# Attention phase: the last context row as a per-channel constant on x, its double stored once, and the weight fold ahead of the sums with x

## The reference, cut to what matters

```python
qf = jnp.fft.fft(q, axis=2); kf = jnp.fft.fft(k, axis=2)        # q = layernorm(x), k = v = ctx
corr = jnp.fft.ifft(qf * jnp.conj(kf), axis=2).real
w, idx = jax.lax.top_k(corr.transpose(0, 1, 3, 2), topk)        # topk = 11 delays per channel
w = jax.nn.softmax(w, axis=-1)
for i in range(topk):
    g = jnp.minimum(idx[:, :, None, :, i] + pos, L - 1)          # past the end: the last row again
    out = out + w[:, :, None, :, i] * jnp.take_along_axis(v, g, axis=2)
x = x + out
```

## Time and profile before

| | before |
|---|---|
| time, median of 3 runs | 3191.58 us (3190.05 to 3197.46) |
| the profiled execution | 3189.48 us, its span 3187.7 us |
| attention phase | the first 1220 us or so of the span |
| PE, DVE, ACT, POOL busy, whole span | 91%, 86%, 71%, 50% |
| granted clock of TensorE, whole span | 0.972 |

### The profile page before, as it was taken

One profiled execution on the slowest core, in us unless ns is written; L12 is line 12 of the kernel. 1 busy time (PEld: TensorE's weight loads), 2 busy tenths in 40 slices (PEclk: granted clock), 3 DMA queues, 4 the chain that ended last, 5 costly groups with the idle time before them and its releaser, 6 DMA issues. The chain is left out here.

```text
span 3187.7 us, 47981 instructions
## 1 busy us (share of the span) xinstructions
PE 2911.0 (91%) x13554; PEld 1586.1 (50%) x13554; DVE 2737.9 (86%) x7168; ACT 2252.5 (71%) x5963; POOL 1581.7 (50%) x1161
## 2 busy tenths in 40 slices
PE   5999999999999996899999999999999999738886
PEld 3666666666666663445444454444445444322322
DVE  4999999999999996776878879787887978769996
ACT  6888888888888862765766767667586766468773
POOL 5999999999999992001212121121212212016776
PEclk8999999999999998999999999999999999859998
DMA  5555555555555535354654737465473744553664
GB/s 174 185 188 167 180 174 161 181 173 160 178 178 160 177 117 173 87 163 126 177 169 136 225 110 214 131 178 163 136 225 103 206 148 132 124 194 147 247 250 162
DMA packets 272044, 532.26 MB, mean 167 GB/s; under 512 B 32664, under 2 KB 132760, under 8 KB 248992
## 3 DMA queue, kind: packets, MB, share of 16 engines
q1 hardware_dynamic: 245600, 422.17, 42.4%
q10 hardware_dynamic: 15168, 71.34, 7.9%
q0 software_dynamic: 11008, 35.66, 3.3%
HBM read 401.07 MB, written 128.02 MB: 166 GB/s over the span
## 5 line engine op out<-in xcount | busy, mean ns | idle before, releaser
L1065 PE MATMUL acc<-xh,wq 128*128 128x512 f16 x4096 | 1205.7, 381 | 46.3 <-DVE x_first L1722 17.1
L1065 PE MATMUL acc<-xl,wq 128*128 128x512 f16 x2048 | 758.9, 380 | 0.0
L1284 ACT ACTIVATE unused<-c_first,minus_guess 128x256 bf16<-128x256 f32 x1024 | 505.2, 494 | 268.5 <-DVE minus_guess L1596 224.5
L1065 PEld LDWEIGHTS acc<-xh,wq 128*128 128x128 f16 x4096 | 399.4, 98 | 532.9 <-DVE x_first L1722 23.3
L994 POOL DMA_DIRECT2D c_first<-ctx_pairs x120 | 66.5, 554 | 857.3 <-DVE mk L1647 846.9
L1065 PEld LDWEIGHTS acc<-xl,wq 128*128 128x128 f16 x2048 | 200.8, 98 | 243.3 <-issue 2.7
L444 PEld LDWEIGHTS bu<-m_iz,zf 128*128 128x128 f32 x2048 | 278.9, 191 | 50.3 <-issue 35.6
L444 PE MATMUL bu<-m_iz,zf 128*128 128x128 f32 (+2 forms) x2048 | 293.0, 301 | 5.5 <-DVE zf L648 5.5
L463 PE MATMUL bx<-m_ic,pf 128*128 128x256 f32 x1024 | 236.1, 384 | 8.9 <-POOL pf L345 8.9
L463 PEld LDWEIGHTS bx<-m_ic,pf 128*128 128x128 f32 x1024 | 192.7, 193 | 34.1 <-POOL pf L345 9.7
L1266 ACT ACTIVATE unread<-cf 128x256 bf16<-128x256 f32 x256 | 106.1, 415 | 127.9 <-DVE feat_pair L1695 94.9
(11 more groups left out here) (359 smaller groups left out, 6975.9 us busy)
## 6 DMA issues: line engine op xcount, KB each, us to landing
wq<-w_split SPq DMA_DIRECT2D x512, 256.0 KB, 3.2
c_first<-ctx SPq DMA_DIRECT2D x64, 512.0 KB, 7.4
xt<-xT SPq DMA_DIRECT2D x64, 512.0 KB, 5.9
x_pairs<-xo SPq DMA_DIRECT2D x64, 512.0 KB, 3.3
c_first<-ctx_pairs POOLq DMA_DIRECT2D x128, 256.0 KB, 4.8
x<-xn_pairs SPq DMA_DIRECT2D x32, 1024.0 KB, 5.4
out_pairs<-ost SPq DMA_DIRECT2D x32, 1024.0 KB, 5.1
x_first<-x SPq DMA_DIRECT2D x15, 2048.0 KB, 8.4
```

What stands on the lines that cost most here:

```text
L1065: return pe.matmul(acc[b][:], ws[(WQ * o + k // CK) % WR][:, k % CK, a, :], x[:, k, :], start=start, stop=False)
L1284: act.activation(signs[:, u // 2, t] if n == COUNTS - 1 else unused[u % 2][:], ct[k % CR][:, t], ACT.Sign, bias=guess[q % 2][:, u:u + 1], ...
```

## The change

The constant that the last row adds to the even part is the same at every time and the weights of a channel sum to one, so it comes out as v_last / 2 on every output of the channel. The changed kernel leaves it out of the spectrum and adds it to x: ScalarE adds a column `lc` (128 partitions, one column per group of 128 channels) to the tile `xt` in four instructions per chunk (`add_last`). The doubled last rows are made once at the start from a new input, stored to a scratch array `last` in DRAM and loaded from there per chunk straight into `vl2`. On VectorE the folds of the weights move ahead of the sums with x; on ScalarE the copy `w_back` moves ahead of the row sums of the weights and both correlation copies move ahead of the squares.

```diff
@@ SyncE, at the start @@
+            sp.dma_start(lr[:], last_in_rows).then_inc(last_in, 16)
+            sp.dma_start(lc[:], last_cols).then_inc(cols_in, 16)
...
+            sp.wait_ge(last_ok, 1)
+            sp.dma_start(last.rearrange("b (a n) -> (b a) n", a=P // NB), lr[:]).then_inc(last_out, 16)
@@ SyncE, each chunk @@
-                        sp.wait_ge(vl2_ok, n_scaled)
-                        sp.wait_ge(ce_ok, n_folded)
-                    sp.dma_start(vl[s][:], ctx[bass.ds(b, 1), L // 2, c * CW:(c + 1) * CW].rearrange("a n -> (a n)").partition_broadcast(P)).then_inc(vl_in[s], 16)
+                        sp.wait_ge(eo_ok, h - 1)
+                        sp.wait_ge(ce_ok, 2 * (h - 1))
+                    else:
+                        sp.wait_ge(last_out, 16)
+                    sp.dma_start(vl2[s], last[bass.ds(b, 1), c * CW:(c + 1) * CW].rearrange("a n -> (a n)").partition_broadcast(P)).then_inc(vl_in[s], 16)
@@ GpSimd, the odd fold @@
-                pool.wait_ge(vl2_ok, h + 1)
+                pool.wait_ge(vl_in[s], 16 * (4 * it + kk // 2 + 1))
@@ TensorE, ahead of the transposes @@
-                        pe.wait_ge(dc_ok, f + 1)
+                        pe.wait_ge(k_sb, f + 1)
@@ ScalarE @@
+            act.wait_ge(last_in, 16)
+            act.activation(lr[:], lr[:], ACT.Copy, scale=2.0).then_inc(last_ok, 1)
+            act.wait_ge(cols_in, 16)
+            act.activation(lc[:], lc[:], ACT.Copy, scale=0.5).then_inc(cols_ok, 1)
+            act.wait_ge(cols_ok, 1)
...
-                act.activation(vl2[s][:], vl[s][:], ACT.Copy, scale=2.0).then_inc(vl2_ok, 1)
+                tile = xt[kk % 2]
+                act.wait_ge(xt_in[kk % 2], 16 * (4 * it + kk // 2 + 1))
+                for j in range(CT):
+                    act.activation(tile[:, j, :], tile[:, j, :], ACT.Identity, bias=lc[:, CT * g + j:CT * g + j + 1]).then_inc(xt_ok, 1)
...
+                if k % CH in (1, 2):
+                    add_last(it, k)
...
+                if k % CH not in (1, 2):
+                    add_last(it, k)
@@ VectorE @@
-                    dve.wait_ge(k_part, 3 * f + 2)
-                    dve.scalar_tensor_tensor(kf[s][0:1, 0, :], vl2[s][0:1, :], L / 2.0, by[0:1, 0, :], ALU.mult, ALU.add).then_inc(dc_ok, 1)
...
+                    for j in range(CT):
+                        dve.wait_ge(xt_ok, CT * g + j + 1)
+                        dve.scalar_tensor_tensor(xo[s][:, j, :], bu[:, j // 2, (j % 2) * L:(j % 2 + 1) * L], wrec[s][:, j:j + 1], xt[s][:, j, :], ALU.mult, ALU.add).then_inc(x1_sum, 1)
```

More of the change, by code:

```diff
@@ L66, in counted, with attention_phase @@
     return n if isinstance(n, int) else eng.snap(eng.to_reg(n))
-def attention_phase(nc, x, ctx, xT, dft, x1, x1_squares, wT, w_rows, w_split, w_sums, w_cols, ctx_pairs, x_first, c_first, ident, vl, v_twice, last_squares, x_in2, c_in2, sums_out):
+def attention_phase(nc, x, ctx, xT, dft, x1, x1_squares, wT, w_rows, w_split, w_sums, w_cols, ctx_pairs, last_in_rows, last, last_cols, x_first, c_first, ident, vl2, last_squares, x_in2, c_in2, sums_out):
     NB, L, D = x.shape
@@ L106, in attention_phase @@
         ce = [sb(f"ce{i}", [P, 3, CW]) for i in range(2)]
-        vl2 = [v_twice, sb("v_last_twice1", [P, CW])]
+        lr, lc = sb("last_rows_sb", [P, NB * D // P]), sb("last_cols_sb", [P, NB * D // P])
         xt = [sb(f"xt{i}", [P, CT, L]) for i in range(2)]
@@ L140, in attention_phase @@
         vl_in = [sem(f"v_last_in{i}") for i in range(2)]
-        ce_ok, vl2_ok, eo_ok, dc_ok = map(sem, ("c_folded", "v_last_twice", "c_odd", "k_mean_ok"))
+        ce_ok, eo_ok, xt_ok = map(sem, ("c_folded", "c_odd", "xt_with_last"))
+        last_in, last_ok, last_out, cols_in, cols_ok = map(sem, ("last_rows_in", "last_rows_twice", "last_rows_out", "last_cols_in", "last_cols_half"))
         cx_in = [sem(f"cx_in{i}") for i in range(2)]
@@ L229, in step @@
                     if least(h, 2):
-                        n_scaled, n_folded = counted(sp, h - 1), counted(sp, 2 * (h - 1))
-                        sp.wait_ge(vl2_ok, n_scaled)
-                        sp.wait_ge(ce_ok, n_folded)
-                    sp.dma_start(vl[s][:], ctx[bass.ds(b, 1), L // 2, c * CW:(c + 1) * CW].rearrange("a n -> (a n)").partition_broadcast(P)).then_inc(vl_in[s], 16)
+                        sp.wait_ge(eo_ok, h - 1)
[3 more added lines that the diff above has]
+                    sp.dma_start(vl2[s], last[bass.ds(b, 1), c * CW:(c + 1) * CW].rearrange("a n -> (a n)").partition_broadcast(P)).then_inc(vl_in[s], 16)
                     sp.dma_start(cx[s][:], ctx[bass.ds(b, 1), :, c * CW:(c + 1) * CW].rearrange("a (t p) n -> p (a t) n", p=P)).then_inc(cx_in[s], 16)
@@ L321, in fold_ctx @@
                 pool.tensor_tensor(ce[s][:, 1, :], cx[s][:, 0, :], cx[s][:, 1, :], ALU.subtract).then_inc(ce_ok, 1)
-                pool.wait_ge(vl2_ok, h + 1)
+                pool.wait_ge(vl_in[s], 16 * (4 * it + kk // 2 + 1))
                 pool.wait_ge(ce_ok, 2 * (h + 1))
-                pool.tensor_tensor(ce[s][:, 2, :], ce[s][:, 0, :], vl2[s][:], ALU.subtract).then_inc(eo_ok, 1)
+                pool.tensor_tensor(ce[s][:, 2, :], ce[s][:, 0, :], vl2[s], ALU.subtract).then_inc(eo_ok, 1)
             def split_step(it, k):
@@ L503, in split_step, with add_last @@
                 act.activation(wp[h % 2][:, :, 0, :], w[:].rearrange("p (j n) -> p j n", n=P), ACT.Copy).then_inc(w_hi, 1)
-            def last_rows(it, k):
-                h = chunk(it, k, AFTER_S)
-                if h is None:
+            def add_last(it, k):
+                g = chunk(it, k, AFTER_I)
+                if g is None:
                     return
[L510 to L515, removed]
-                act.activation(vl2[s][:], vl[s][:], ACT.Copy, scale=2.0).then_inc(vl2_ok, 1)
+                kk = k - AFTER_I
+                tile = xt[kk % 2]
+                act.wait_ge(xt_in[kk % 2], 16 * (4 * it + kk // 2 + 1))
+                for j in range(CT):
+                    act.activation(tile[:, j, :], tile[:, j, :], ACT.Identity, bias=lc[:, CT * g + j:CT * g + j + 1]).then_inc(xt_ok, 1)
             def mean(it, k, a):
@@ L562, in step @@
                 normalize(it, k)
[L563 to L566, removed]
                 split_step(it, k)
@@ L612, in step @@
                     act.activation(xo[s][:, :, 0:P - 1], bu[:].rearrange("p b (h t) -> p (b h) t", h=2)[:, :, 0:P - 1], ACT.Copy).then_inc(odd_sb, 1)
+                if k % CH not in (1, 2):
+                    add_last(it, k)
                 mean(it, k, 0)
                 squares(it, k, 0)
+                if t is not None:
+                    act.wait_ge(t_mm, t + 1)
+                    if least(t, 1):
+                        act.wait_ge(fold_ok, 2 * t)
+                    act.activation(wb[:], by[:, 1, :], ACT.Copy).then_inc(wb_sb, 1)
                 h = chunk(it, k, AFTER_W + 1)
@@ L619, in step @@
                     act.activation(w[:], w[:], ACT.Copy, scale=W_SCALE, accum_out=wrow[:, h:h + 1]).then_inc(w_summed, 1)
[L620 to L624, removed]
                 if f is not None and least(f, 2):
@@ L627, in step @@
                 correlations(f, 0)
+                correlations(f, 1)
                 if g is not None:
@@ L631, in step @@
                     act.activation(xt[s][:], xo[s][:], ACT.Square).then_inc(sq1_ok, 1)
-                correlations(f, 1)
             steps(step)
@@ L706, in step @@
                     dve.wait_ge(q_mm, f + 1)
-                    dve.wait_ge(k_part, 3 * f + 2)
-                    dve.scalar_tensor_tensor(kf[s][0:1, 0, :], vl2[s][0:1, :], L / 2.0, by[0:1, 0, :], ALU.mult, ALU.add).then_inc(dc_ok, 1)
                     if least(f, 1):
                         dve.wait_ge(p_sum, 2 * f)
-                    dve.wait_ge(dc_ok, f + 1)
                     dve.wait_ge(k_part, 3 * f + 3)
@@ L735, in step @@
                     dve.tensor_tensor(plus, plus, odd, ALU.add).then_inc(joined_ok, 1)
[L736 to L743, removed]
                 if t is not None:
@@ L750, in step @@
                     dve.tensor_tensor(we[:, 1, :], by[:, 0, :], wb[:], ALU.subtract).then_inc(fold_ok, 1)
+                if g is not None:
+                    kk = k - AFTER_I
+                    s = kk % 2
+                    dve.wait_ge(joined_ok, g + 1)
+                    if least(g, 2):
+                        dve.wait_ge(x1_out[s], 16 * (4 * it + kk // 2))
+                        dve.wait_ge(added_ok, g - 1)
+                    dve.wait_ge(w_rec, g + 1)
+                    for j in range(CT):
+                        dve.wait_ge(xt_ok, CT * g + j + 1)
+                        dve.scalar_tensor_tensor(xo[s][:, j, :], bu[:, j // 2, (j % 2) * L:(j % 2 + 1) * L], wrec[s][:, j:j + 1], xt[s][:, j, :], ALU.mult, ALU.add).then_inc(x1_sum, 1)
                 if f is not None:
@@ L2527, in autocorrelation_lora_ffn_channel_attention_experts @@
     masks = scratch("mask_pairs", pairs_shape, UINT8)
```

(5 more changed lines are left out.)

## The result

| | before | after |
|---|---|---|
| time, median | 3191.99 us (3190.05 to 3197.46, 4 runs) | 3224.73 us (3219.12 to 3229.26, 4 runs) |
| the profiled execution | 3189.48 us, span 3187.7 | 3219.12 us, span 3217.3 |
| ratio to before, 95% interval | | 1.0102 (1.009 to 1.0113) |

What follows compares the result with a forecast made beforehand. VectorE, TensorE and GpSimd were nearly full, with the attention step set by the loop through folds, `bu` and `xo`. Terms -10 - 4 - 0.5 = -14.5 on 3189.5 gave 3175, as median 3177 us; range 3164 to 3189.

Steps and rivals of the forecast that it cites:

- first loop: Attention step: folds, TensorE's spectra and `bu`, `xo` copy, sums with x; 18.29 us before, 16.7 claimed after.
- The walk: Four attention steps (one batch) followed with ScalarE executing in order: 72.9 us instead of 73.6, 0.7 gained a batch.
- step C: Third of the four attention steps walked: `xo` at 37.0 us behind X, `w_back` 39.1, folds 39.7, sums with x 40.9.
- The wait for `w_back`: VectorE in the attention steps: expected to wait some 0.5 to 0.9 us a step for ScalarE's copy.
- The sum's term of -10: Attention phase: 0.7 us gained for each batch, over 14 batches 10 us.
- The price of an add: ScalarE's adds with a column as bias: four take 1.62 us, at least 1.6, at most 1.98.
- The start: First context load issued at about 13.5 us, not 7.31; GpSimd starts 0 to 2 us later; term taken as -0.5.
- The last steps: Last six attention steps, without mean or squares: about 17.6 us each, 4 us gained.
- "Slower": Rival on ScalarE: dear adds, 2.8 us for four, each batch 1.7 us longer, 3212 us; chance 0.08.

Runs made afterwards that it cites:

- e1: The changed kernel with the copy `w_back` on ScalarE right behind the `xo` copy, ahead of late adds, mean and squares of x: 3174.12 us, ratio 0.9953 to before.
- e4: The kernel before with the new order alone on VectorE and ScalarE, no constant and no adds: 3201.82 us, ratio 1.0034 to before.
- e6: The changed kernel with `w_back` right behind `xo` and VectorE's second pair of maxima moved behind prod_o: 3153.73 us, ratio 0.9885 to before.
- e3: The changed kernel without the 256 adds of the constant on ScalarE: 3199.45 us, ratio 1.0034 to before.
- e5: The changed kernel with `w_back` right behind `xo` and without the 256 adds on ScalarE: 3164.98 us, ratio 0.992 to before.
- e7: The kernel before with only VectorE's second pair of maxima moved behind prod_o: 3208.64 us, ratio 1.0055 to before.
- e2: The changed kernel with VectorE's sums with x ahead of the folds again, ScalarE keeping its adds and order: 3186.53 us, ratio 0.9993 to before.

## Why the prediction was wrong

**The step that failed** is in the part on VectorE: "The folds go ahead of L743, which takes 1.58 out of the loop: 16.7. Both make TensorE and GpSimd the bound, at 17.4 to 17.5, if ScalarE keeps up." It holds for the first loop alone. TensorE's code waits for `ze_mul` ahead of `by` and for `zo_mul` ahead of `bz`; no row of before shows these waits, since the products were done 0.3 to 0.9 us earlier, and I took what the trace didn't show as what didn't bind. The timelines of before had the answer:

```profile
619.33 1.21 DVE L642 TENSOR_TENSOR prod_o<-bz,vf 128x1024 f32<-128x1024 f32 x1
...
620.88 1.88 PE L404 MATMUL bz<-ce,m_o 128*128 128x512 f32 x4
```

prod_o ends at 620.54, 0.34 before the `bz` that had to wait for it, and by these 0.34 the second loop is shorter than the first (18.29 less 17.96 is 0.33). The loop through the products is 18.0, not 16.7, so the order could win 0.3 us a step and not 0.9, and every wait that it uncovered counted in full. e1, e4 and e6 show it from three sides.

**The walk** carried that into the numbers. Behind X (the `xo` copy at 624.82) L759 starts at 4.2, the squares at 5.9 and `kf` at 13.3, where I had 4.2, 5.9 and 13.4; L726 comes at 17.9 (18.1), the folded weights at 23.9 (23.6). ScalarE's part was right. From step C on it fails: I let TensorE run on with `bz` and `bu` as soon as it was through with the folded weights, while it waited for the products. The next `xo` came at 38.6 instead of 37.0, and four steps became 76.0 us, not 72.9.

**The wait for `w_back`** was in my walk (named under "What will show it" with 0.5 to 0.9 a step; it came at 0.65, 0.95, 0.65 and 1.37), but priced at nothing, since VectorE seemed to have room: 17.1 of its own work against 17.5. In the second loop it has none. The sum's term of -10 had the wrong sign: the 55 full steps lost 31.6 us.

**The price of an add** was right: 256 adds of 495 ns, and 1.60 us from the first of four to the `kf` copy (636.49 to 638.09) where I took 1.62. But they cost 20 to 25 us in the changed kernel (e3), for the most part because the two late groups stand ahead of `w_back`, and 6 to 10 where nothing waits for it (e5). The walk has both places, but in a loop that seemed 0.9 us a step shorter than it was, where they could only eat into a gain.

**The start**: the first context fold of GpSimd came at 20.03, 3.7 later than 16.32 and beyond the 0 to 2 that I estimated. The load was issued at 13.04, where I had 13.5, but its first user started 7.0 us later, and I had counted on a short queue. The DMA engines were down to 0.4 to 0.5 of their time between 15 and 17 us, yet the load took as long as its like in the kernel before (7.4 from issue to landing, median). Only 0.8 of it reached the first L719, so the term of -0.5 became +0.8. **The last steps** were to bring 4 us, at 17.6 each. Of the last four two took 17.96 and two 18.7, 73.4 in all against 73.2 before: the term came to nothing.

**The rivals.** "Slower" was given 0.08, with dear adds as its mechanism; the time was slower by another one. The chance was too small because no rival was a longer loop of waits: all were cases of ScalarE's load or of the start.

**Open.** e1 and e5 stand 0.17 and 0.10 us a step above the 17.96 of the second loop. A late correlation copy (0.26 us in one step of four of e5) is part of it, in e1 a late `kf` as well; the rest was not taken apart.

## What to carry to other kernels

When an instruction is moved out of a loop of waits, list every wait in the code that guards a buffer it shares with other engines, also those that the trace never shows as waits: each may close a loop of its own, and the next longest is the new step. How long such a loop is can be read before the change: if nothing else in it waits, it is the step less the time by which the awaited result was early. Then ask of every copy that used to be ready in time what covered it; here 1.6 us of sums hid a copy that stood behind a mean or squares, and 50 us hung on its place in ScalarE's order. And the same move can gain in one order (e6) and lose in another (e7): an instruction that is in no loop may still fill a gap.

## What the runs showed of the hardware

The same instruction on VectorE (128x1024, `bx` times `kf`) takes 1223 to 1225 ns in every instance between 300 and 1000 us before, and 1204 to 1226 with a median of 1207 after. Its median is 1223 or 1224 in the six kernels that have L708 right ahead of it, 1204 to 1210 in five of the six that have not, and 1225 in the sixth (e2). What shortens it was not tried. At 0.02 us an instruction it is far below the differences above.
